# K and u exchange their homes in SBUF, the K and V weights load inside the FFN, and x is stored after the last gather

## The reference, cut to what matters

```python
x = x + attn_a(layernorm(x))          # mixes over the batch, one scan over features
x = x + ffn(layernorm(x))             # first FFN block: 1024 of 2048 tokens pass
x = x + attn_b(layernorm(x))          # delta-rule attention, then a gated MLP
x = x + ffn(layernorm(x))             # second FFN block, the same weights

def ffn(h):                           # Mixture-of-Depths, D = 1024, F = 4096
    scores = h @ w_router
    top_scores, top_idx = top_k(scores, S // 2)
    sel = h[top_idx]
    y = gelu(sel @ W1 + b1) @ W2 + b2
    return h.at[top_idx].add(sigmoid(top_scores) * y)

def attn_b(x):
    h = rmsnorm(x)
    k = normalize(h @ Wk);  v = ema_scan(h @ Wv);  q = h @ Wq
    ...                               # beta, delta scan over tokens, Wo, residual
    ...                               # rmsnorm, silu(h2 @ w_gate) * (h2 @ w_up) @ w_down
```

## Time and profile before

| What | Value |
|---|---|
| Time, median of 3 runs | 2024.6 us (2019.87 to 2028.94) |
| Profiled execution, its own time | 2015.21 us |
| Its span on the slowest core (core 1), the one read below | 2013.6 us |
| Spans of the 8 cores | 1996.0 to 2013.6 us |
| Mean granted TensorE clock by core | 0.932 to 0.937 |
| PE busy | 1692.2 us, 84% of the span |
| DVE, ACT, POOL busy | 885.8, 691.2, 196.4 us |
| q0 (software DMA queue) | 94.76 MB, 26.6% of 16 engines' span |
| q1 (hardware DMA queue) | 104.88 MB, 15.6% of 16 engines' span |
| Chain that ended last | PE 76%, DMA 10%, DVE 7%, issue 3% |

### The profile page before, as it was taken

The page is one execution under the profiler, slowest core; times in us unless marked ns, Lnnn a source line. Parts: engine busy times, 40 slices in busy tenths (PEclk is TensorE's granted clock), DMA queues, the critical chain, the costliest instruction groups (busy, mean ns, idle before and its releaser), DMA issues.

```text
span 2013.6 us, 23643 instructions; the slowest of 8 cores (1996.0 to 2013.6 us)
## 1 busy us (share of the span) xinstructions
PE 1692.2 (84%) x8330; PEld 803.3 (40%) x8330; DVE 885.8 (44%) x1699; ACT 691.2 (34%) x1051; POOL 196.4 (10%) x272
## 2 busy tenths in 40 slices
PE   1999999671499992799999999999999995279997
PEld 0444444231344441354454444444444442144443
DVE  4788887387322213526442432442222355611222
ACT  4788886057311232420233322341000110722112
POOL 2212121021200013100000000000000100200002
PEclk9999999795699995899999999999999998589998
DMA  9776673484233469920010100373025322064445
GB/s 275 212 230 210 209 233 102 77 157 83 82 60 67 83 115 227 245 41 1 1 43 4 40 21 22 70 136 57 1 48 90 64 52 52 35 227 74 84 84 84
DMA packets 69426, 201.16 MB, mean 100 GB/s; under 512 B 4606, under 2 KB 4670, under 8 KB 69312
## 3 DMA queue, kind: packets, MB, share of 16 engines
q0 software_dynamic: 40960, 94.76, 26.6%
q1 hardware_dynamic: 28352, 104.88, 15.6%
HBM read 228.97 MB, written 33.59 MB: 130 GB/s over the span
## 4 chain that ended last, share of the span: by engine, by line
PE 76%; DMA 10%; DVE 7%; issue 3%; DVEq 1%; ACT 1%; POOL 1%; another core or an unknown queue 0%; ACTq 0%; SPq 0%; POOLq 0%
PE v_h1ps L969 11%; PE v_h2ps L981 10%; PE yps L478 10%; PE mlp_a L1652 5%; PE ab_bank L1487 5%; PE mlp_a L1640 5%; PE ab_bank L1525 3%; PE qps L499 3%; PE ab_bank L1431 3%; PE ab_bank L1438 3%; PE ab_big L1412 3%; PE mlp_a L1666 3%; PE mlp_r L1666 3%; PE ab_bank L1381 2%; DMA x_tok<-upd_dram,idx_add 2%
## 5 line engine op out<-in xcount | busy, mean ns | idle before, releaser
L478 PE MATMUL yps<-ring,diag 128*128 128x512 f32 x512 | 225.4, 598 | 12.1 <-POOL diag L374 12.1
L981 PE MATMUL v_h2ps<-m_w,m_h1q 128*128 128x512 bf16 x1024 | 222.3, 379 | 0.0
L969 PE MATMUL v_h1ps<-m_sel_fm,m_w 128*128 128x512 bf16 x1024 | 222.3, 379 | 0.0
L916 ACT ACTIVATE m_h1q<-v_h1ps,fb_s 128x512 bf16<-128x512 f32 x128 | 87.7, 687 | 294.4 <-PE v_h1ps L969 294.4
L889 DVE TENSOR_TENSOR m_acc<-v_h2ps,m_acc 128x512 f32<-128x512 f32 x96 | 66.3, 691 | 262.0 <-PE v_h2ps L981 262.0
L547 DVE SCALAR_TENSOR_TENSOR scr_v<-ring,wvs_bc 128x1024 bf16<-128x1024 f32 x128 | 152.6, 1211 | 0.6 <-issue 0.4
L981 PEld LDWEIGHTS v_h2ps<-m_w,m_h1q 128*128 128x128 bf16 x1024 | 100.0, 98 | 121.0
L969 PEld LDWEIGHTS v_h1ps<-m_sel_fm,m_w 128*128 128x128 bf16 x1024 | 100.3, 98 | 120.2
L478 PEld LDWEIGHTS yps<-ring,diag 128*128 128x128 f32 x512 | 96.7, 192 | 128.5 <-issue 128.5
L1624 ACT ACTIVATE gate_prod<-mlp_a 128x512 bf16<-128x512 f32 x64 | 38.2, 597 | 272.1 <-PE mlp_a L1640 271.9
L1640 PE MATMUL mlp_a<-xln_fm,wg_buf 128*128 128x512 bf16 x512 | 112.1, 379 | 2.6 <-ACT gate_prod L1624 2.6
(11 more groups left out here) (263 smaller groups left out, 2260.0 us busy)
## 6 DMA issues: line engine op xcount, KB each, us to landing
ring<-x_all SPq DMA_DIRECT2D x64, 1024.0 KB, 6.7
m_w<-fW POOLq DMA_DIRECT2D x16, 2048.0 KB, 14.1
x_tok<-x_all POOLq DMA_DIRECT2D x16, 512.0 KB, 7.5
y_dram<-x_tok SPq DMA_DIRECT2D x4, 2048.0 KB, 19.9
x_tok<-y_dram SPq DMA_DIRECT2D x16, 512.0 KB, 4.3
x_tok<-y_dram POOLq DMA_DIRECT2D x16, 512.0 KB, 5.4
out<-x_tok SPq DMA_DIRECT2D x4, 2048.0 KB, 20.9
m_sel_tok<-sel_dram SPq DMA_DIRECT2D x8, 514.0 KB, 6.0
```

Of the source, the lines that this page charges most:

```text
L478: ii = t.matmul(yps[tt % 2][:, h * 512:(h + 1) * 512], lhsT=diag_of(n), rhs=x_tile(n)[:, h * 512:(h + 1) * 512], start=(n % B == 0), stop= ...
L916: s.activation(out=h1q[:, ft * D + h * 512:ft * D + (h + 1) * 512], in_=h1ps[n % 4][:, :], func=AF.Gelu_apprx_tanh, bias=fb1_s[:, q * 8 + ...
L969: ii = t.matmul(h1ps[n % 4][:, :], lhsT=w1[:, dt * D + ft * P:dt * D + (ft + 1) * P], rhs=sel_fm[:, dt * D + h * 512:dt * D + (h + 1) * 51 ...
L981: ii = t.matmul(h2ps[m % 4][:, :], lhsT=h1q[:, ff * D + rt * P:ff * D + (rt + 1) * P], rhs=w2[:, ff * D + h * 512:ff * D + (h + 1) * 512], ...
```

## The change

K and u change places, and with them all that lies over them: `k_fm`, `xfm16` and the second FFN block's `xn` and `acc` go from 98 to 34 KiB; `u_tok` goes from 34 to 98; the second FFN block's W1 and W2 buffers go from 34 and 50 to 98 and 114. The buffers bwk and bwv go to 100 and 116, which in the first FFN block hold the router's work arrays (`sdg`, `cmp`, `r_bc`) and the bias `b2_bc`. The bias is last read by the first 16 evictions of results, so the load of the V weights has a wait on `h2ev` = 16. Attention b's two rotating tiles `rot_b` (130) are replaced by `m_rot` (32 and 134.25), which the MLP stage uses already.

On POOL the load of the K weights and five small loads of vectors are issued in the FFN's loop behind the load of W2's quarter 1, and the load of the V weights behind that of W2's quarter 2. On SP all 8 waits on gathered updates stand ahead of the first x store, in place of two waits ahead of each.

```diff
--- before.py
+++ after.py
@@ -260,7 +260,7 @@
 
     def at_kib(name, shape, dtype, kib):
         return nc.alloc_sbuf_tensor_at(name, list(shape), dtype, offset=arena + int(kib * 1024))
-    xfm16 = at_kib('xln_fm', (P, ND * T), BF16, 98)
+    xfm16 = at_kib('xln_fm', (P, ND * T), BF16, 34)
     wg_buf = at_kib('wg_buf', (P, ND * D), BF16, 66)
     xb16 = at_kib('gate_prod', (P, 8192), BF16, 82)
     wu_buf = at_kib('wu_buf', (P, ND * D), BF16, 16)
@@ -270,10 +270,10 @@
     dot_scrs = [[dot_scr[:, 0:D], dot_scr[:, D:2 * D]], [m_rot[0][:, :], m_rot[1][:, :]]]
     r_bcs = [at_kib('r_bc', (P, D), F32, 120), at_kib('r_bc1', (P, D), F32, 130.25)]
     b2_bcs = [at_kib('b2_bc', (P, D), F32, 124), at_kib('b2_bc1', (P, D), F32, 84)]
-    bwk = at_kib('bwk', (P, ND * D), BF16, 34)
-    bwv = at_kib('bwv', (P, ND * D), BF16, 50)
+    bwk = at_kib('bwk', (P, ND * D), BF16, 100)
+    bwv = at_kib('bwv', (P, ND * D), BF16, 116)
     MOD_AT = [dict(xn=0, acc=0, sel_fm=34, w1=50, sel_tok=66, h1q=66, w2=84, sdg=100, cmp=108),
-              dict(xn=98, acc=98, sel_fm=0, w1=34, sel_tok=66, h1q=66, w2=50, sdg=16, cmp=24)]
+              dict(xn=34, acc=34, sel_fm=0, w1=98, sel_tok=66.25, h1q=66.25, w2=114, sdg=16, cmp=24)]
     MOD_SHAPE = dict(xn=((P, NT * SELW), BF16), acc=((P, 8 * D), F32), sel_fm=((P, ND * D), BF16), w1=((P, ND * D), BF16),
                      sel_tok=((P, 8 * SELW), BF16), h1q=((P, 8 * D), BF16), w2=((P, ND * D), BF16), sdg=((P, T), F32), cmp=((P, 2 * T), BF16))
     mod_buf = [{nm: at_kib(f'm{inv}_{nm}', MOD_SHAPE[nm][0], MOD_SHAPE[nm][1], kib) for nm, kib in MOD_AT[inv].items()} for inv in range(2)]
@@ -752,15 +752,17 @@
                 g.wait_ge(sem(V + 'h2mm'), at(V + 'h2mm', 16 * q))
                 g.dma_start(out=w2[:, :].rearrange('p (k n) -> p k n', k=ND),
                             in_=wD['fW2'].rearrange('(k p) n -> p k n', p=P)[:, q * ND:(q + 1) * ND, :]).then_inc(sem(V + 'ldw2'), 16)
+                if inv == 0 and q == 1:
+                    g.dma_start(out=bwk[:, :].rearrange('p (k n) -> p k n', k=ND), in_=wD['bWk'].rearrange('(k p) n -> p k n', p=P)).then_inc(sem('ab_wk_ld'), 16)
+                    g.dma_start(out=n1w, in_=wD['b_n1']).then_inc(sem('ab_vecs'), 16)
+                    g.dma_start(out=n2w, in_=wD['b_n2']).then_inc(sem('ab_vecs'), 16)
+                    g.dma_start(out=alph, in_=wD['b_alpha']).then_inc(sem('ab_vecs'), 16)
+                    g.dma_start(out=btw, in_=wD['b_betaw']).then_inc(sem('ab_vecs'), 16)
+                    g.dma_start(out=swv_tmp[0:1, 0:1], in_=wD['b_betab']).then_inc(sem('ab_vecs'), 16)
+                if inv == 0 and q == 2:
+                    g.wait_ge(sem(V + 'h2ev'), at(V + 'h2ev', 16))
+                    g.dma_start(out=bwv[:, :].rearrange('p (k n) -> p k n', k=ND), in_=wD['bWv'].rearrange('(k p) n -> p k n', p=P)).then_inc(sem('ab_wv_ld'), 16)
             if inv == 0:
-                g.wait_ge(sem(V + 'h1mm'), at(V + 'h1mm', 64))
-                g.dma_start(out=bwk[:, :].rearrange('p (k n) -> p k n', k=ND), in_=wD['bWk'].rearrange('(k p) n -> p k n', p=P)).then_inc(sem('ab_wk_ld'), 16)
-                g.dma_start(out=n1w, in_=wD['b_n1']).then_inc(sem('ab_vecs'), 16)
-                g.dma_start(out=n2w, in_=wD['b_n2']).then_inc(sem('ab_vecs'), 16)
-                g.dma_start(out=alph, in_=wD['b_alpha']).then_inc(sem('ab_vecs'), 16)
-                g.dma_start(out=btw, in_=wD['b_betaw']).then_inc(sem('ab_vecs'), 16)
-                g.dma_start(out=swv_tmp[0:1, 0:1], in_=wD['b_betab']).then_inc(sem('ab_vecs'), 16)
-                g.dma_start(out=bwv[:, :].rearrange('p (k n) -> p k n', k=ND), in_=wD['bWv'].rearrange('(k p) n -> p k n', p=P)).then_inc(sem('ab_wv_ld'), 16)
                 g.wait_ge(sem('zrow'), at('zrow', 16))
                 g.wait_ge(sem(V + 'gidx'), at(V + 'gidx', 4))
                 for tt in range(NT):
@@ -1033,12 +1035,11 @@
         NSB = 4
         v_fm = at_kib('v_fm', (P, ND * T), BF16, 0)
         q_fm = at_kib('q_fm', (P, ND * T), BF16, 0)
-        u_tok = at_kib('u_tok', (P, NT * D), BF16, 34)
+        u_tok = at_kib('u_tok', (P, NT * D), BF16, 98)
         h_fm = at_kib('h_fm', (P, ND * T), BF16, 66)
         gq3 = at_kib('gq3', (P, 16384), BF16, 66)
-        k_fm = at_kib('k_fm', (P, ND * T), BF16, 98)
+        k_fm = at_kib('k_fm', (P, ND * T), BF16, 34)
         inv_mt = at_kib('inv_mt', (P, NT * P), BF16, 130)
-        rot_b = at_kib('rot_b', (P, 2 * D), BF16, 130)
         xt16 = x_tok.bitcast(BF16)
         bwo = xt16[:, 0:8192]
         bwq = xt16[:, 8192:16384]
@@ -1127,9 +1128,9 @@
         def attn_b_sync(s):
             xv_ = x_tok[:, :].rearrange('p (tt d) -> p tt d', tt=NT)
             yv_ = y_dram.ap().rearrange('(tt p) d -> p tt d', p=P)
+            for k in range(8):
+                s.wait_ge(sem(V + f'xin{k}'), at(V + f'xin{k}', 32))
             for j in range(4):
-                for k in (2 * j, 2 * j + 1):
-                    s.wait_ge(sem(V + f'xin{k}'), at(V + f'xin{k}', 32))
                 s.dma_start(out=yv_[:, 4 * j:4 * j + 4, :], in_=xv_[:, 4 * j:4 * j + 4, :]).then_inc(sem(V + f'xst{j}'), 16)
             for j in range(4):
                 s.wait_ge(sem(V + f'xst{j}'), at(V + f'xst{j}', 16))
@@ -1288,7 +1289,7 @@
                     s.wait_ge(sem(V + 'asc'), at(V + 'asc', tt // 4 + 1))
                 if tt >= 2:
                     s.wait_ge(sem(V + 'htr'), at(V + 'htr', tt - 1))
-                s.activation(out=rot_b[:, tt % 2 * D:(tt % 2 + 1) * D], in_=x_tok[:, tt * D:(tt + 1) * D], func=AF.Identity,
+                s.activation(out=m_rot[tt % 2][:, :], in_=x_tok[:, tt * D:(tt + 1) * D], func=AF.Identity,
                              scale=asc[:, tt:tt + 1], bias=bsc[:, tt:tt + 1]).then_inc(sem(V + 'hem'), 1)
 
             def k_evict(n):
@@ -1367,7 +1368,7 @@
                 if tt >= 2:
                     t.wait_ge(sem(V + 'hev'), at(V + 'hev', tt - 1))
                 for dt in range(ND):
-                    ii = t.transpose(out=htr[tt % 2][:, dt * P:(dt + 1) * P], in_=rot_b[:, tt % 2 * D + dt * P:tt % 2 * D + (dt + 1) * P],
+                    ii = t.transpose(out=htr[tt % 2][:, dt * P:(dt + 1) * P], in_=m_rot[tt % 2][:, dt * P:(dt + 1) * P],
                                      identity=cS['ident16'][:, :])
                 ii.then_inc(sem(V + 'htr'), 1)
 
```

## The result

Against the kernel before, the changed kernel took 0.983 of the time, 95% interval 0.980 to 0.986: from a median of 2024.5 us to 1989.7, the middle of its three undisturbed executions (1988.95, 1989.69, 1990.88). Two more, at 2063 us, are left out, since the cores of one die ran at a lower clock in them. The forecast was 1993 us, range 1981 to 2007. Two repeats, each on a chip of its own, gave 0.988 (0.986 to 0.990) and 0.987 (0.984 to 0.990); on the chip of the second the kernel before against itself gave 0.998 (0.996 to 1.000), 4 us from 1. So the change is worth some 24 to 35 us, and a single comparison is good to 4 us at best.

What follows compares the result with a forecast made beforehand. Late gathers behind the K and V weights were taken to bound the passage after the FFN. Gather 11 landing at 789 instead of 820.6 gave 31.7 us, so 2024.6 - 31.7 = 1993 us, range 1981 to 2007.

Steps and rivals of the forecast that it cites:

- K+: Time from TensorE's last FFN matmul to the K projection's start; forecast about 15.5 us, before 39.4.
- Part 1: Loading K and V weights inside the FFN: gather 11 lands at 789 us, TensorE resumes 31.7 us earlier.
- V+: Time from TensorE's last FFN matmul to the V projection's start; forecast about 95.7 us, before 127.4.
- the restart: TensorE resuming in the K projection after its last long gap: forecast 794.7 us, before 826.37, then 62.2 us to V.
- slack of 1.3 us: In the K projection, gather 11 lets TensorE resume at 794.7 us, 1.3 after its own work runs dry.
- Part 2: The two weight loads in the FFN's idle queue time: cost nothing, hidden by 12 us of slack.
- Part 3: x stores behind all gathers on SP: cost nothing, slack 65 us; gathers 3.05 us each instead of 3.87.
- Part 4: Exchanged buffer homes and m_rot: same shapes, partitions and number of instructions, so no effect.
- A: Rival, chance 0.10: engines do not limit gathers, which land at POOL's 1.83 us pace; gain 33 to 37, time 1989.
- B: Rival, chance 0.13: gathers after the FFN still cost 3.87 us each; gain 20 to 24 us, time 2003.
- C: Rival, chance 0.03: x stores and Wo take the weights' place later, VectorE waits at 916 us; time 2024.
- D: Rival, chance 0.04: K and V loads starve W1's quarters 2 and 3 in the FFN; time 2035 us.

Runs made afterwards that it cites:

- Three loads in a row: Changed kernel with both the K and V weight loads issued behind W2's quarter 1; ratio 0.986 (0.983 to 0.989) to the kernel before.
- both edits: Changed kernel with VectorE's statistics of tiles 0 to 3 moved behind result 63 and another order of evictions and roots; ratio 0.988 to the kernel before.

## Why the prediction was right, point by point

**What bound the passage** was read rightly: weights ahead of gather 0, VectorE standing for it in front of results 61 to 63. With the loads moved alone, K+ fell from 39.0 to 20.2.

**Part 1, a size off.** Forecast for core 1: K+ 15.5, V+ 95.7. Measured: 21.0 and 97.2; over the cores 20.5 and 99.5. The step that was mis-sized is "I take 4.25" for a gather with its store, and with it "they land at 749, 753, 757.5, 761.5": gather 3 landed at 759.14 + 9.34 = 768.5, 5.6 us after the FFN's end, where I had it 0.3 us after. The working took an update store to land in 3 to 4 us; row tile 3's took 7.0 beside the gathers, with the engines 90% busy in these 7 us. The trace of before had the warning: the first store of row tiles took 8.6 us there, beside the weights. So a wait of 6.48 us was left where I wrote that four statistics follow at once, and row tile 7 came 5.4 us late.

Two errors the other way gave most of it back. A gather costs 2.66 us, not 3.05, so gather 11 landed 31.9 us after the FFN's end against 27.8. (The working's own steps of 3.05 us from 776 lead to 788.2 and not to 789, which the sum used.) And the stretch from the restart to V, which I left at 62.2 us, took 860.15 - 800.86 = 59.3, since more of it ran at 2.4 GHz: the 16 K matmuls behind the restart took 3.62 us instead of 6.19, the last 64 took 13.99 instead of 15.67, and 16 in between 5.30 instead of 3.62. The first may come from the shorter wait before it, which is argued and not tested. The 1.7 us of the last 64 are luck of this core: on five of the others they took 15.67 as before. So V's 1.5 us off on core 1 is a 5.5 us error at K with most of it cancelled, not a sum that held term by term.

The slack of 1.3 us by which gather 11 was to set the restart was about nil. VectorE's wait for the root ahead of tile 4's eviction is 0.40 us when gather 11 comes last, as in the trace of before; in the changed kernel it is longer on four of the eight cores, core 1 among them, so TensorE's and ScalarE's own work ended last there. From the timelines of DVE, core 1, first before, then changed:

```profile
824.71 0.17 DVE L707 COPY yst_ag<-a_dotw 128x4 f32<-128x4 f32 x1 [0.40 <-ACT a_dotw L702]
```

```profile
799.20 0.17 DVE L707 COPY yst_ag<-a_dotw 128x4 f32<-128x4 f32 x1 [0.76 <-ACT a_dotw L702]
```

The windows of the changed kernel, core 1, against the earlier trace rows:

```profile
763.00:780.00 17.00, 2.02 (x16) 1.55 (x16) 5.64 (x19) 7.54 (x8) 5.96 (x4) 0.58 0.83 185
780.00:801.00 21.00, 14.79 (x75) 7.05 (x76) 17.00 (x43) 8.70 (x12) 11.14 (x8) 0.77 1.01 198
801.00:827.00 26.00, 23.45 (x137) 11.36 (x136) 13.96 (x26) 11.71 (x16) 1.20 (x2) 0.93 0.96 234
827.00:860.00 33.00, 33.00 (x292) 17.76 (x292) 5.23 (x6) 14.50 (x22) 0.70 (x1) 1.00 0.95 216
```

**A base that flattered the gain.** All terms were taken from core 1, where V+ was 127.4; the mean over the cores was 125.6. The gain in V+ is 30 us on core 1 and 26 in the mean, against 31.7. The timed base flattered it too: the profiled executions alone went from 2015.21 to 1988.95 us, 26.3 us, as the passage did, while the forecast started from the timed median, 9.4 us above the profiled execution, and the changed kernel's median lies only 0.7 us above its own. So the passage gave 5.7 us less than forecast in the mean, the timed gain 9 us more than the passage, and that 1989.7 falls 3 us from 1993 is partly luck.

**Part 2 held.** The pair took 28.7 us (28.3 forecast), W1's quarter 2 was issued before its end and W1 waited for nothing. In order of service one detail was off: W2 landed in 17.5 us instead of 14.1 with K's load behind it. Three loads in a row found the edge of the slack where it was put, within 2 us.

**Part 3 held in its cost, not in its share.** No engine waited for x stores behind the last gather: Wo landed at 847.6, 72 us before its use, and Wq, issued at 826.77, 31.7 us later at 858.5 (851 forecast for the last). How the gain divides was not seen: the sum gave 24 us to the loads and the other 7.7 to the stores and group 1's wait. Measured, the loads alone give 15.5 us and the stores alone 4; on top of the other, each gives more, the stores 10.6 and the loads 22.

**Part 4 held** in time (0.998 with the homes alone).

**The rivals.** A, gathers at POOL's pace, is out: whole gathers fill q0 (101.9%), and halving them moved V by 6.4 us. The rate that the Trainium skill gives in DMA: Bandwidth & Descriptors (anatomy of a DMA on the software path), bytes over 436 GB/s, would be 1.2 us for a gather; the 1.56 us for its bytes and 1.1 us beside them are well above. B, 3.87 us for each, is out: 2.66. C and D did not happen: no engine waited for Wo or for W1.

**Left open:** why the timed gain was 35 us in the first comparison and 24 to 27 in the two repeats, when the passage gave 24 to 26 in every profile and the stretch behind it stayed (the kernel before against itself differs by 4 us, which is about half of it); the 12 us timed with the stores alone, where the passage gave 4; and the 2.6 us of V+ with the homes alone.

## What to carry to other kernels

A load that is not needed yet but is issued ahead of something that is can cost most of its own length: 28 us of weights in front of the first gather held VectorE, through it the last results, their stores and the later gathers, and cost 15.5 us of the passage by themselves, 22 with the x stores out of the way. Look at what a queue still holds when a short, urgent DMA joins it, and move the long one into a stretch where the queue is idle, after working out which load of that stretch it then delays. Two moves that free the same resource do not add up singly (15.5 and 4.1 us of 26), so measure them together too.

## What the hardware showed that I had not expected

- A store of 0.5 MB on the hardware queue, 3.0 us alone, took 7.0 beside gathers on the software queue. Over its own 7 us (751.27 to 758.29, core 1, changed kernel) the two queues together filled 90% of the engines' time, over the whole stretch from 740 to 765 us only 78%:

```profile
q0 software_dynamic: 163, 0.60, 52.8%
q1 hardware_dynamic: 295, 1.07, 37.4%
```

- A gather that adds into SBUF cost 2.66 us of all engines, and 1.88 at half the bytes; a straight line through the two sizes leaves about 1.1 us that does not shrink with its bytes (an estimate).
- TensorE's clock can fall while it is busy throughout. Behind 128 matmuls of one column (3.3 us) the last 64 of the K projection took 13.99 us in the changed kernel and 16.89 us with both edits, core 1; in these windows the granted clock was 1.00 and 0.82 (2.4 GHz throughout, and 1.2 GHz for a part). On five other cores of the changed kernel they took 15.67. The small matmuls stand ahead in all these cases, so that they are the cause is not shown:

```profile
846.20:860.00 13.80, 13.80 (x66) 6.26 (x66) 0.33 (x2) 5.74 (x10) 0.00 (x0) 1.00 0.79 141
```

```profile
845.40:862.20 16.80, 16.80 (x66) 7.07 (x66) 0.33 (x2) 5.74 (x10) 0.00 (x0) 0.82 0.77 114
```
